# Expert blocks with the up products turned round: weights stationary, rows moving

## What is computed

```
# each token goes to the 2 best of E = 8 experts; D = 256, F = 512
mid = einsum('ead,edf->eaf', routed_in, w_in)
sw  = einsum('ead,edf->eaf', routed_in, w_swiglu)
h   = silu(mid) * sw
out = einsum('eaf,efd->ead', h, w_out)
```

## Time and profile before

| | us |
|---|---|
| median of 3 runs | 3273.63 |
| lowest and highest | 3271.70, 3276.22 |
| span of the profiled execution | 3276.1 |
| expert blocks in it (first turn to last product) | 790.9 to 1208.4 |
| mean granted TensorE clock | 0.975 |

### The profile page before, as it was taken

How to read it: one execution, slowest core, us unless ns; L and a number is a source line. 1 busy time by engine, 2 the same in 40 slices (tenths; PEclk the granted TensorE clock), 3 DMA queues, 4 the chain that set the end, 5 groups by cost and what they waited for, 6 DMA issues and landing times. The chain is left out here.

```text
span 3276.1 us, 46433 instructions
## 1 busy us (share of the span) xinstructions
PE 3113.6 (95%) x15196; PEld 1806.9 (55%) x15197; DVE 1926.4 (59%) x4751; ACT 1678.1 (51%) x3775; POOL 703.1 (21%) x847
## 2 busy tenths in 40 slices
PE   8899998788999989999998999999999999999999
PEld 4455555455666654333332666666555666666555
DVE  6999996333111125665664687777332677777342
ACT  5666662221222224666665688887221677776221
POOL 1000001543000013554543222222000212121111
PEclk9999999889999999999998999999999999999999
DMA  9800004103111120111100100000000100000000
GB/s 334 294 1 1 1 1 143 45 26 102 46 45 45 45 89 21 29 29 29 30 19 16 34 11 10 11 9 5 28 1 1 42 8 11 10 9 5 14 14 26
DMA packets 114254, 134.08 MB, mean 41 GB/s; under 512 B 14479, under 2 KB 100343, under 8 KB 113787
## 3 DMA queue, kind: packets, MB, share of 16 engines
q1 hardware_dynamic: 106042, 109.54, 10.3%
q0 software_dynamic: 7872, 21.77, 2.1%
q10 hardware_dynamic: 128, 0.10, 0.0%
HBM read 60.30 MB, written 60.83 MB: 37 GB/s over the span
## 5 line engine op out<-in xcount | busy, mean ns | idle before, releaser
L1801 DVE CUSTOM_DVE_ANT_0 sb_win_masked<-ps_win_pss,sb_win_around 128x384 f32<-128x384 f32 (+1 forms) x512 | 256.3, 537 | 177.7 <-PE ps_win_pss L1929 175.1
L2468 PE MATMUL ps_stk_banks<-sb_stk_w,sb_loc_hT 128*128 128x512 f32 x768 | 352.2, 609 | 2.7 <-ACT sb_loc_hT L2208 2.7
L2241 ACT ACTIVATE sb_loc_pr<-ps_loc_psw,sb_loc_nb,sb_loc_sc 128x256 f32<-128x256 f32 x512 | 281.0, 569 | 135.6 <-DVE sb_loc_nb L2386 135.6
L1663 ACT ACTIVATE sb_win_pT<-ps_win_pst 128x512 f32<-128x512 f32 x368 | 199.8, 596 | 176.7 <-PE ps_win_pst L1940 122.0
L1929 PE MATMUL ps_win_pss<-sb_win_kT,sb_win_q 32*128 32x384 f32 (+1 forms) x1024 | 234.1, 528 | 31.4 <-DVE sb_win_qtok L1801 20.4
L2468 PEld LDWEIGHTS ps_stk_banks<-sb_stk_w,sb_loc_hT 128*128 128x128 f32 x768 | 142.8, 193 | 180.1 <-issue 180.1
L749 PE MATMUL ps_rec_psp<-sb_rec_hT,sb_rec_w 128*128 128x512 f32 x512 | 234.7, 602 | 0.8 <-DVE sb_keep_modf L504 0.8
L1940 PE MATMUL ps_win_pst<-sb_win_qm,sb_win_kT 32*128 32x512 f32 x736 | 217.5, 665 | 1.5 <-ACT sb_win_pT L1663 1.5
L2763 DVE SCALAR_TENSOR_TENSOR sb_mlp_hid<-ps_stk_banks,sb_stk_col,sb_mlp_gl 128x512 f32<-128x512 f32 (+1 forms) x112 | 75.1, 672 | 244.6 <-ACT sb_mlp_gl L2718 244.4
L1352 DVE TENSOR_TENSOR sb_exp_hid<-ps_exp_ps,sb_exp_act_f 128x512 f32<-128x512 f32 x71 | 49.1, 691 | 277.4 <-PE ps_exp_ps L1386 277.4
L1586 POOL TENSOR_SCALAR_AFFINE_SELECT sb_win_pT<-sb_win_pT 128x512 f32<-128x512 f32 x240 | 146.5, 634 | 255.0 <-ACT sb_win_pT L1663 255.0
(11 more groups left out here) (363 smaller groups left out, 6822.9 us busy)
## 6 DMA issues: line engine op xcount, KB each, us to landing
sorted_tokens<-sb_rec_blank SPq DMA_DIRECT2D x9, 4224.0 KB, 30.2
sb_exp_rows<-sorted_tokens SPq DMA_DIRECT2D x71, 128.0 KB, 2.0
expert_results<-sb_exp_res SPq DMA_DIRECT2D x71, 128.0 KB, 1.7
sb_moe_w_in<-in_L_ffn_w_in_eDF SPq DMA_DIRECT2D x8, 512.0 KB, 10.6
sb_moe_w_sw<-in_L_ffn_w_swiglu_eDF SPq DMA_DIRECT2D x8, 512.0 KB, 10.6
sb_exp_w_out<-in_L_ffn_w_out_eFD POOLq DMA_DIRECT2D x8, 512.0 KB, 9.1
sb_stk_angles<-in_angles SPq DMA_DIRECT2D x32, 128.0 KB
sb_stk_xs_b<-sb_stk_y SPq DMA_DIRECT2D x64, 63.5 KB
```

The costliest lines, as they stand in the source:

```text
L1663: nc.scalar.activation(pT[:, n % PARTS], pst[:, n % TURNED], ACT.Exp, scale=SC).then_inc(s_e, 1)
L1801: nc.vector.tensor_tensor_reduce(masked[:, pair % 2, j, 0:keys], pss[:, (n + j) % PLAIN, 0:keys], around[:, first:first + keys], 1.0, -3e3 ...
L2241: e = nc.scalar.activation(pr[:, hf, h], psw[:, hf, h // 2, h % 2 * 256:h % 2 * 256 + 256], ACT.Exp, scale=sc8[:, b, hh:hh + 1], bias=nb[: ...
L2468: t = nc.tensor.matmul(psa[:, c], hT[:, b, k, 1 - k:P + 1 - k], w[:, k, c * 512:(c + 1) * 512], start=(k == 0), stop=(k == KD - 1))
```

## The change

The weights of the block's expert are copied to a fixed place, `here` [128, 2, 2, 1024]: those of `w_in` by ScalarE (`fetch_in`), those of `w_sw` by VectorE (`fetch_sw`), each with a `value_load` of its own and one copy of 128 x 1024 from SBUF to SBUF. In `up` a 128 x 128 piece of these weights is stationary and the 128 turned rows move; each bank of `ps` is filled in four pieces of 128 columns, with two products each, and then holds the middle tile with F on partitions. So `hid` has the layout that `down` wants: `turn_hidden`, `hidden`, `hidT` and `psh` go. `up` has no `value_load` of its own any more, and waits for the copies instead. The wait for the loaded weights moves from TensorE to ScalarE and VectorE.

```diff
+                def fetch_in(base, k):
+                    e = act.value_load(t["block_expert"][0:1, bass.ds(base + k, 1)], min_val=0, max_val=EXP)
+                    if k >= 2:
+                        act.wait_ge(s_mid, base + k - 1)
+                    nc.scalar.copy(here[:, k % 2, 0], w_in[:, bass.ds(e, 1)].rearrange("p a c f -> p (a c f)")
+                                   ).then_inc(s_in_here, 1)
+
+                act.wait_ge(t["w_here"], 16 * 2 * EXP)
+                fetch_in(0, 0)
                 rows_in(0, 0)
                 rows_in(0, 1)
+                fetch_in(0, 1)
                 silu(0, 0)
 
                 def step(base, k):
-                    hidden(base, k - 1)
                     if not (isinstance(base, int) and k + 1 >= XBLOCKS):
                         rows_in(base, k + 1)
+                        fetch_in(base, k + 1)
                     silu(base, k)
...
+                def fetch_sw(base, k):
+                    e = dve.value_load(t["block_expert"][0:1, bass.ds(base + k, 1)], min_val=0, max_val=EXP)
+                    if k >= 2:
+                        dve.wait_ge(s_sw, base + k - 1)
+                    nc.vector.tensor_copy(here[:, k % 2, 1], w_sw[:, bass.ds(e, 1)].rearrange("p a c f -> p (a c f)")
+                                          ).then_inc(s_sw_here, 1)
...
                 def step(base, k):
+                    if not (isinstance(base, int) and k + 1 >= XBLOCKS):
+                        fetch_sw(base, k + 1)
                     product(base, k)
                     result(base, k - 1)
...
                 def up(base, k):
-                    e = pe.value_load(t["block_expert"][0:1, bass.ds(base + k, 1)], min_val=0, max_val=EXP)
                     pe.wait_ge(s_xT, base + k + 1)
-                    for j, (wt, done) in enumerate(((w_in, s_mid), (w_sw, s_sw))):
-                        for c in range(KD):
-                            i = nc.tensor.matmul(ps[:, k % 2, j], xT[:, k % 2, c],
-                                                 wt[:, bass.ds(e, 1), c].rearrange("p a f -> p (a f)"),
-                                                 start=(c == 0), stop=(c == KD - 1))
+                    for j, (ready, done) in enumerate(((s_in_here, s_mid), (s_sw_here, s_sw))):
+                        pe.wait_ge(ready, base + k + 1)
+                        for f in range(KF):
+                            for c in range(KD):
+                                i = nc.tensor.matmul(ps[:, k % 2, j, f * P:(f + 1) * P],
+                                                     here[:, k % 2, j, c * FF + f * P:c * FF + (f + 1) * P],
+                                                     xT[:, k % 2, c], start=(f == 0 and c == 0),
+                                                     stop=(f == KF - 1 and c == KD - 1), skip_group_check=True)
                         i.then_inc(done, 1)
-
-                def turn_hidden(base, k):
-                    pe.wait_ge(s_hid, base + k + 1)
-                    for f in range(KF):
-                        i = nc.tensor.transpose(psh[:, f * P:(f + 1) * P], hid[:, k % 2, f * P:(f + 1) * P], ident[:])
-                    i.then_inc(s_hturned, 1)
...
                 def step(base, k):
-                    turn_hidden(base, k - 1)
                     if not (isinstance(base, int) and k + 1 >= XBLOCKS):
                         turn(base, k + 1)
                     up(base, k)
                     down(base, k - 1)
```

More of the change, by code:

```diff
@@ L1260, in run_experts @@
         hid = m.sb("hid", [P, 2, FF])
-        hidT = m.sb("hidT", [P, 2, FF])
         res = m.sb("res", [P, UNROLL, D])
+        here = m.sb("here", [P, 2, 2, KD * FF])
         psx = m.ps("psx", [P, 512])
         ps = m.ps("ps", [P, 2, 2, FF])
-        psh = m.ps("psh", [P, FF])
+        psw = m.ps("psw", [P, FF])
         pso = m.ps("pso", [P, 512])
-        s_turned, s_xT, s_mid, s_sw, s_silu, s_hid, s_hturned, s_hidT, s_out, s_res = (
-            m.sem(n) for n in "turned xT mid sw silu hid hturned hidT out res".split())
+        s_turned, s_xT, s_mid, s_sw, s_silu, s_hid, s_out, s_res, s_in_here, s_sw_here = (
+            m.sem(n) for n in "turned xT mid sw silu hid out res w_in_here w_sw_here".split())
         s_wo = keep["soft"].sem("w_out_in")
@@ L1328, in silu @@
                     nc.scalar.activation(act_f[:, k % 2], ps[:, k % 2, 0], ACT.Silu).then_inc(s_silu, 1)
-                def hidden(base, k):
-                    act.wait_ge(s_hturned, base + k + 1)
-                    nc.scalar.copy(hidT[:, k % 2], psh[:]).then_inc(s_hidT, 1)
+                def fetch_in(base, k):
[6 more added lines that the diff above has]
+                fetch_in(0, 0)
                 rows_in(0, 0)
                 rows_in(0, 1)
+                fetch_in(0, 1)
                 silu(0, 0)
                 def step(base, k):
-                    hidden(base, k - 1)
                     if not (isinstance(base, int) and k + 1 >= XBLOCKS):
                         rows_in(base, k + 1)
+                        fetch_in(base, k + 1)
                     silu(base, k)
                 pipeline(act, step)
-                hidden(0, XBLOCKS - 1)
             @block.vector
@@ L1359, in result @@
                     nc.vector.tensor_copy(res[:, k % UNROLL], pso[:, 0:D]).then_inc(s_res, 1)
+                def fetch_sw(base, k):
[4 more added lines that the diff above has]
+                                          ).then_inc(s_sw_here, 1)
+                dve.wait_ge(t["w_here"], 16 * 2 * EXP)
+                fetch_sw(0, 0)
+                fetch_sw(0, 1)
                 product(0, 0)
                 def step(base, k):
+                    if not (isinstance(base, int) and k + 1 >= XBLOCKS):
+                        fetch_sw(base, k + 1)
                     product(base, k)
@@ L1381, in up @@
                 def up(base, k):
-                    e = pe.value_load(t["block_expert"][0:1, bass.ds(base + k, 1)], min_val=0, max_val=EXP)
                     pe.wait_ge(s_xT, base + k + 1)
-                    for j, (wt, done) in enumerate(((w_in, s_mid), (w_sw, s_sw))):
-                        for c in range(KD):
-                            i = nc.tensor.matmul(ps[:, k % 2, j], xT[:, k % 2, c],
-                                                 wt[:, bass.ds(e, 1), c].rearrange("p a f -> p (a f)"),
-                                                 start=(c == 0), stop=(c == KD - 1))
-                        i.then_inc(done, 1)
-                def turn_hidden(base, k):
-                    pe.wait_ge(s_hid, base + k + 1)
-                    for f in range(KF):
-                        i = nc.tensor.transpose(psh[:, f * P:(f + 1) * P], hid[:, k % 2, f * P:(f + 1) * P], ident[:])
-                    i.then_inc(s_hturned, 1)
+                    for j, (ready, done) in enumerate(((s_in_here, s_mid), (s_sw_here, s_sw))):
[6 more added lines that the diff above has]
+                                                     stop=(f == KF - 1 and c == KD - 1), skip_group_check=True)
+                        i.then_inc(done, 1)
                 def down(base, k):
                     e = pe.value_load(t["block_expert"][0:1, bass.ds(base + k, 1)], min_val=0, max_val=EXP)
-                    pe.wait_ge(s_hidT, base + k + 1)
+                    pe.wait_ge(s_hid, base + k + 1)
                     if k:
@@ L1404, in down @@
                     for f in range(KF):
-                        i = nc.tensor.matmul(pso[:, 0:D], hidT[:, k % 2, f * P:(f + 1) * P],
+                        i = nc.tensor.matmul(pso[:, 0:D], hid[:, k % 2, f * P:(f + 1) * P],
                                              w_out[:, bass.ds(e, 1), f].rearrange("p a f -> p (a f)"),
@@ L1408, in down @@
                     i.then_inc(s_out, 1)
-                spin(nc, ident, psh, 16)
-                pe.wait_ge(t["w_here"], 16 * 2 * EXP)
+                spin(nc, ident, psw, 16)
                 turn(0, 0)
@@ L1423, in _ @@
                 pipeline(pe, step)
-                turn_hidden(0, XBLOCKS - 1)
                 down(0, XBLOCKS - 1)
```

## The result

The changed kernel takes 3241.4 us (median of 4 runs, 3238.6 to 3250.3) against 3272.7 for the kernel before: a ratio of 0.9908, with a 95% interval of 0.9892 to 0.9923. It is 31.3 us faster, where 21.6 were forecast. The direction was right, the size was not: 3241.4 lies 1.6 us under the range.

A forecast was written before the change was run, and what follows sets the result against it. TensorE was taken as the bound, a pure stream of matmuls in the expert blocks. Per block -0.44 + 0.15 = -0.29 us, 71 blocks -20.6, edges -1.0: -21.6, giving 3252 us; range 3243 to 3272.

The forecast's parts named there:

- items 1 and 2: Per block on TensorE: removing four middle-tile turns saves 0.44 us; `up` as 32 pairs at 0.112 adds 0.15.
- the edges: Start and end of the expert stage: a 0.85 us wait goes, the last product starts 0.6 earlier; together 1.0 us.
- Items 3 to 6: TensorE's sequencing, ScalarE's copy (1.05 us), VectorE's copy (1.22 taken) and later waits all stay hidden, costing nothing.
- rival C: TensorE's longer loop code is fetched anew, giving back 14 to 27 us: 3266 to 3279; chance 0.06.
- A: In `up`, weight loads are partly exposed, losing beyond 0.121 us a pair; at 0.141, +45 us, 3319; chance 0.12.
- B: TensorE's queue runs dry, exposing the register load of `down`: 32 us added, 3284; chance 0.04.
- the sum: Whole program: -0.29 us per block over 71 blocks, plus edges, is -21.6 us, giving 3252.0.

The follow-up runs named there:

- half_columns: Changed kernel with every second product of each piece in `up` moving 64 columns instead of 128, all loads kept; one execution 3247.0 us, step 5.52.
- spare_turns: Changed kernel with four unused turns in each of 70 steps, where the middle tile's turns stood; median 3274.9 us, 3274.6 at clock 0.978.
- one_expert: Changed kernel without both weight copies and their register loads, `up` reading expert 0's weights in place; 3246.4 us, 3244.7 at clock 0.978.
- copies_on_act: Changed kernel with both weight copies on ScalarE and none on VectorE; median 3250.1 us, 3242.8 at clock 0.978.
- before_delay10: Kernel before with 92 unused turns behind the expert stage's last product; median 3269.2 us, 3273.8 at clock 0.978.

## Why the prediction was off

**The step of a block (items 1 and 2) was right.** 5.53 was forecast, 5.52 measured; the pair 0.112 and 0.112. The row that priced it was of loads with two moving columns, and `half_columns` shows that this was the right row to take, for the right reason. The turn's 0.109, the lower bound, would have given 7 us too much.

**The stage was right.** -20.6 and -1.0 for the edges were forecast, -21.9 measured in the first pair of traces. At the end TensorE waits 0.71 us for `result(69)` before the last product. The forecast's "within 0.8 us of the one before it" holds from the end of that one; from start to start it is 2.60. That the removed turns are worth their full time, with no slack behind them, `spare_turns` shows: 30.6 us for 30.6.

**Items 3 to 6 were right.** The ScalarE copy took 1.05; the VectorE copy 0.70, below the 1.22 that I took and near the lower end. `one_expert` and `copies_on_act` show that both are free, and that ScalarE could take another copy of 1.04 us. That no engine took TensorE's place shows in the windows. No row says which of the two instruction queues is the matmul engine's, as the prediction had it, but between 850 and 1150 us neither moved a packet, though the loop had grown (rival C):

```profile
q1 hardware_dynamic: 15696, 14.29, 15.0%
```

**The rivals.** A (a load partly exposed) decides at 0.121, and the load came at 0.112. The Trainium skill's factor for a stream of pairs at 128 columns (TensorE: Matmul & The Clock Gate, section Back-to-back issue gap) would have made it 0.158; this trace doesn't show it, and the measurement decides. B didn't happen: no idle time before `up` or `down`.

**What failed is the last sentence of the sum,** "The clock's low stretches around the stage may fall 1 or 2 us otherwise". That term was mis-sized. By the common line the clock's part is (0.9790 - 0.9765) x 2500 = 6 us over all executions, and 31.3 - 23.6 = 8 us in the first comparison. The sum had carried over the clock of the kernel before unchanged, and gave it 1 or 2 us with no row behind that size, though the page showed low digits in the routing and in the windowed attention; two hundredths of clock in that last stage are 8.5 us. With a term of 6 to 8 us below, the range would have held the time. Two smaller parts of the 10.6 us between 3252.0 and 3241.4: the 3273.6 that the sum started from was the median of three runs, and over 66 it is 3271.1; and at equal clock the change is worth 23.6 +- 1.7 us, so that the forecast's 21.6 lies 0.3 us outside the lower end of that.

**What stays open.** Why the clock in the windowed attention is what it is for a given timing stays open. `before_delay10` shows that the kernel before gets the better clock without the change, and `copies_on_act` that a kernel with the new `up` can be without it, so the 6 to 8 us are no merit of the new `up`. But no run here says which timing is good, and I wouldn't trust another change that shifts the stages to keep them.

## What to carry to other kernels

When TensorE is busy for the whole of a stage, price each kind of pair by the distance of two starts, and check that the sum closes on the step; here this forecast the step of a restructured product to 0.01 us. With smaller moving pieces, ask for the distance of bare weight loads: for float32 it was 0.112 us, and a piece of 128 columns (0.107) lies just under it, so that a smaller piece still costs the full 0.112. Compare kernels at equal granted clock, and where stages behind the change run below full clock, put the swing of the clock in the range, as a shift in time alone can move it.

## What the runs showed of the hardware

- A shift in time changes the mean clock: that of the kernel before rose from 0.9765 to 0.9791 with a delay of 7.6 us ahead of the windowed attention. The same matmuls of that stage were busy for 561.0 us in one execution and 544.7 in one of another kernel; single executions of one kernel differ nearly as much in clock, 0.974 to 0.980. Over all kernels 0.001 of mean clock is 2.5 us.
- In a stream of float32 loads of 128 columns a pair took 0.112 or 0.113 us with 2, 8 or 128 moving columns, and with 64 and 128 in turn; at 256 it took 0.216.
- VectorE copies 1024 float32 per partition from SBUF to SBUF in 0.697 us, where an operation with two operands takes 1.221; ScalarE takes 1.047 for the same copy.
